# The Down stage of a gated block: H quantised in small parts by VectorE, later tiles turned by DMA in halves

## The chip, the core and the metric

The kernel runs on one core of a Trainium2 chip. The engines named are TensorE (PE, matmuls and transposes), VectorE (DVE), ScalarE (ACT), GpSimd (POOL) and SyncE (SP), which issues the DMAs. The metric is device time of one execution in microseconds, the median of the runs.

## The reference, cut to what matters

```python
x = x + tanh(g_xattn) * matmul(fake_quant(layernorm(x)), fake_quant(ctx))
# the block's second half, on layernorm(x) as A:
gate, up = A @ Wg.T * g, A @ Wu.T * g              # A fp8-quantised, W int4-quantised
h = silu(gate) * up                                # 1024 x 2752
gm = max(max(abs(h)) / (448 * 6), 1e-8)            # one number for all of h
xr = h / gm
# blocks of 16 columns; the last 128 columns are quantised twice
def fp8_block_qdq(v):
    s = max(max(abs(vb)) / 448, 1e-8)              # one per block vb
    return float8_e4m3(vb / s) * s
Am = concat(fp8_block_qdq(xr[:, :n]), q1, q2)      # q1 = qdq(outl), q2 = qdq(outl - q1)
y = Am @ Wd.T * gm                                 # Wd int4-quantised, 1024 wide
out = x + tanh(g_ffn) * y
```

All of h must exist before gm does, and gm before any column of Am. Both index arrays are the identity in the data that is timed; code under `mid_moved > 0` is not executed.

## The kernel before, in words

Rows are worked in 8 tiles of 128. The gate and up products come in column units of 256; in the last unit, eight pieces of H (128x256) are made by TensorE, ScalarE (silu) and VectorE (`make_h`, L1311), and VectorE takes the maxima of blocks of 16 (`max_h`, L1316) into `hm`. H goes to memory by DMA and is read back tile by tile into `h_in` (two slots, `load_tile`, L412).

The Down stage starts when the last maxima are there. VectorE reduces all of `hm` to one number per row (L1407), GpSimd takes the maximum over the partitions (L601), VectorE makes scales from it (L1409 to L1411). Then, for each tile: `scale_h` keeps the outlier columns (L1431) and makes the blocks' scale and coefficient (L1232 to L1235); GpSimd multiplies the tile by the coefficients (`h_times_coef`, L607), except the first 8 groups of 128 columns of tile 0, which VectorE multiplies (L1256); `round_scaled` rounds to fp8 precision with a power of two added and taken off (L1238, L1239, L1240, L1246) and multiplies by the scale (L1247); `quantise_twice` treats the 128 outlier columns (L1263 to L1270).

TensorE turns the quantised tile, 22 transposes of 128x128 (L869) in groups of four into a PSUM bank `tb`; ScalarE copies a group out as f16, the high half (L693), and VectorE subtracts that from the bank, the low half (L1173). `down` then multiplies: 22 column groups, two halves of 512 output columns, three products each (high-high, high-low, low-high), so 132 matmuls a tile (L977). `finish` (L1478) adds the result to the residual, and SP stores it. Tile t+1 is turned between the two output halves of tile t. The order is written out by hand, for each engine; an engine carries out its list in order, and semaphores order the engines: `am_ready` (parts quantised), `lo_done` (groups split), `y_done` (an output half multiplied), `y_out` (result taken, bank free), `turned`, `h_loaded`.

Each step of VectorE's quantisation waits for the one before it on its own semaphore. The transposing DMA is used for the weights already: `turn_gate_up` (L424, 16 blocks of 128x128 f16 per DMA) and `turn_down` (L433, mostly 8).

## Time and profile before

| | us |
|---|---|
| median of 3 runs | 937.62 |
| lowest, highest | 936.37, 938.55 |
| profiled execution | 939.1 |
| its span, first to last instruction | 937.3 |
| busy in the span: TensorE, VectorE | 784.9, 643.9 |
| busy in the span: GpSimd, ScalarE | 337.1, 263.3 |

Shares over the whole span mix stages with different limits; the Down stage is the part from about 646 us to the end. The trace gives each instruction's start and length, what it sat idle for before it, and which engine's event ended that idle time.

### The profile page before, as it was taken

The page shows a single profiled execution, that of the slowest core. Times are in us where ns is not written, and L with a number is a line of the kernel's source. Part 1 is how long each engine was busy: PE and PEld are TensorE (multiplying, and loading weights), DVE is VectorE, ACT ScalarE, POOL GpSimd, SP SyncE. Part 2 cuts the span into 40 slices and gives each one's busy share as a digit, 9 for nine tenths or more (in the row PEclk, how much of TensorE's full clock was granted, in tenths as well). Part 3 has the DMA queues.
Part 4 walks back from the last instruction along what each step waited for, and adds up shares of the span by engine and source line. Part 5 has one row for each costly group of instructions (what it writes and reads, how often), then busy time and mean ns, then how long its engine had stood idle before and what let it go on. Part 6 is the DMA issues. An engine that isn't in the chain of part 4 may idle for free.

```text
span 937.3 us, 11305 instructions
## 1 busy us (share of the span) xinstructions
PE 784.9 (84%) x3808; PEld 377.3 (40%) x3808; DVE 643.9 (69%) x1023; ACT 263.3 (28%) x368; POOL 337.1 (36%) x175
## 2 busy tenths in 40 slices
PE   0698100679999999999999999995589979999998
PEld 0243100445554444444444444442245434444443
DVE  5999789978767566666757667414988695976510
ACT  1964420232235353343425343300001111011000
POOL 1002054854227485665757576500302222112000
PEclk9999555789999999999999999998789999999999
DMA  7633300110038997979788897704011221121100
GB/s 288 209 103 146 130 0 0 45 62 22 20 112 184 214 196 158 221 175 224 169 198 195 194 209 167 176 28 182 1 60 61 106 104 47 60 105 45 45 23 22
DMA packets 144675, 110.32 MB, mean 118 GB/s; under 512 B 117632, under 2 KB 128896, under 8 KB 143616
## 3 DMA queue, kind: packets, MB, share of 16 engines
q1 hardware_dynamic: 144640, 109.88, 44.4%
q8 instruction: 18, 0.29, 0.1%
q14 instruction: 17, 0.14, 0.0%
HBM read 61.88 MB, written 19.66 MB: 87 GB/s over the span
## 4 chain that ended last, share of the span: by engine, by line
PE 69%; DVE 24%; issue 2%; ACT 2%; DMA 1%; POOL 1%; SPq 1%; DVEq 0%; ACTq 0%
PE acc L927 44%; PE acc L977 22%; PE tb L869 2%; DVE mid L1173 2%; DVE big L1240 1%; DVE wbuf L1167 1%; DVE bst L1065 1%; DVE h_in L1247 1%; DVE big L1095 1%; DVE h_in L1239 1%; DMA big<-in_x_dram 1%; DVE h_in L1238 1%; DVE h_in L1185 1%; DVE w_max L1155 1%; DVE h_in L1240 1%
## 5 line engine op out<-in xcount | busy, mean ns | idle before, releaser
L927 PE MATMUL acc<-mid 128*128 128x512 f16 (+1 forms) x2112 | 448.4, 375 | 0.0
L927 PEld LDWEIGHTS acc<-mid 128*128 128x128 f16 x2112 | 207.3, 98 | 239.3 <-issue 1.9
L977 PE MATMUL acc<-big,mid 128*128 128x512 f16 x1056 | 234.6, 385 | 5.2 <-DVE mid L1173 5.2
L544 POOL TENSOR_TENSOR wbuf<-wbuf,w_inv 128x1024 f32<-128x1024 f32 (+1 forms) x68 | 128.4, 1894 | 156.4 <-DVE w_inv L1161 156.4
L977 PEld LDWEIGHTS acc<-big,mid 128*128 128x128 f16 x1056 | 104.4, 99 | 132.6 <-issue 6.8
L583 POOL TENSOR_TENSOR h_in<-wbuf,h_in 128x1024 f16<-128x1024 f32 (+1 forms) x56 | 114.5, 2044 | 87.1 <-ACT h_in L784 86.9
L1311 DVE SCALAR_TENSOR_TENSOR h_out<-acc,gs,silu 128x256 f32<-128x256 f32 (+1 forms) x88 | 41.5, 471 | 119.3 <-ACT silu L742 98.3
L693 ACT ACTIVATE mid<-tb 128x512 f16<-128x512 f32 (+1 forms) x88 | 44.9, 571 | 256.4 <-PE tb L869 234.6
L607 POOL TENSOR_TENSOR h_in<-h_in,mid 128x2752 f32<-128x2752 f32 (+1 forms) x8 | 38.3, 4794 | 166.6 <-DVEq L1438 159.5
L687 ACT ACTIVATE wbuf<-wbuf 128x1024 f32<-128x1024 f32 (+1 forms) x68 | 69.1, 1017 | 99.6 <-POOL wbuf L544 98.8
L1155 DVE TENSOR_REDUCE tb<-wbuf 128x64 f32<-128x1024 f32 (+1 forms) x56 | 65.4, 1169 | 42.0 <-DMA wbuf<-in_L_ffn_w_gate_dram 23.5
L784 ACT ACTIVATE h_in<-wbuf 128x1024 f16<-128x1024 f32 (+1 forms) x56 | 57.1, 1019 | 114.9 <-DVE wbuf L1167 114.9
L1173 DVE TENSOR_TENSOR mid<-tb,mid 128x512 f16<-128x512 f32 (+1 forms) x88 | 51.9, 647 | 45.0 <-ACT mid L693 44.7
L1167 DVE SCALAR_TENSOR_TENSOR wbuf<-wbuf,tb 128x1024 f32<-128x1024 f32 (+1 forms) x56 | 65.1, 1163 | 0.3 <-issue 0.2
L742 ACT ACTIVATE silu<-acc,gs 128x256 f32<-128x256 f32 (+1 forms) x88 | 40.0, 456 | 88.8 <-PE acc L927 88.8
L869 PE MATMUL tb<-ident,big 128*128 128x128 f32 x64 | 10.9, 343 | 57.2 <-DVE big L1270 50.9
L869 PE MATMUL tb<-ident,h_in 128*128 128x128 f32 x176 | 24.6, 287 | 25.6 <-DVEq L1457 16.4
L1478 DVE SCALAR_TENSOR_TENSOR mid<-acc,gs,mid 128x512 f32<-128x512 f32 x16 | 11.5, 748 | 41.2 <-PE acc L977 39.0
L855 PE MATMUL acc<-mid,big 128*128 128x512 bf16 x128 | 32.2, 410 | 4.6 <-DVE big L1095 4.6
L1316 DVE TENSOR_REDUCE hm<-h_out 128x256 f32 (+2 forms) x88 | 34.0, 387 | 2.7
L869 PEld LDWEIGHTS tb<-ident,big 128*128 128x128 f32 x64 | 10.0, 182 | 58.1 <-DVE big L1270 51.5
L869 PEld LDWEIGHTS tb<-ident,h_in 128*128 128x128 f32 x176 | 20.1, 145 | 31.1 <-issue 19.9
(141 smaller groups left out, 594.6 us busy)
## 6 DMA issues: line engine op xcount, KB each, us to landing
h_in<-h_d SPq DMA_DIRECT2D x8, 1376.0 KB, 6.0
wbuf<-in_L_ffn_w_gate_dram SPq DMA_DIRECT2D x21, 512.0 KB, 4.3
wbuf<-in_L_ffn_w_up_dram SPq DMA_DIRECT2D x21, 512.0 KB, 4.1
h_d<-h_out SPq DMA_DIRECT2D x80, 128.0 KB, 3.4
wbuf<-in_L_ffn_w_down_dram SPq DMA_DIRECT2D x16, 512.0 KB, 4.3
wbuf<-in_ctx_dram SPq DMA_DIRECT2D x12, 512.0 KB, 4.4
big<-in_x_dram SPq DMA_DIRECT2D x8, 512.0 KB, 8.2
x_d<-big SPq DMA_DIRECT2D x8, 512.0 KB, 4.0
```

The source lines that it names most:

```text
L544: pool.tensor_tensor(w, w, spread(w_inv[0:rows, b, 0:cols // BLK]), ALU.mult).then_inc(w_scaled, 1)
L583: pool.tensor_tensor(nat[s % 4][:, H:H + cols], wbuf[:, s % 4, 0:cols], nat[s % 4][:, 0:cols], ALU.subtract)\
L687: act.activation(wbuf[0:rows, b, 0:cols], wbuf[0:rows, b, 0:cols], ACT.Copy, bias=MAGIC, scale=W_UP)\
L693: act.activation(dst, tb[bank][:, 0:n * P].rearrange("p (k r) -> p k r", k=n)[:, :, 0:width], ACT.Copy).then_inc(hi_done, 1)
L784: act.activation(nat[s % 4][:, 0:cols], wbuf[:, s % 4, 0:cols], ACT.Copy).then_inc(nat_hi, 1)
L869: last = pe.transpose(tb[bank][:, q * P:q * P + rows], src[0:rows, k * P:(k + 1) * P], ident[0:rows, 0:rows])
L927: last = pe.matmul(acc[m % 4][:, 0:cols], left[:, k, s * P:(s + 1) * P], ring[:, slot, right, k, 0:cols], start=(k == 0 and left is a_hi a ...
L977: last = pe.matmul(acc[2 * i + hf][:], amT[:, i, left, k, :], right[:, k, hf * MW:(hf + 1) * MW], start=(k == 0 and left == 0 and right is ...
L1155: dve.tensor_reduce(top, blocks(wbuf[0:rows, b, 0:cols]), AX_X, ALU.max, apply_absolute_value=True).then_inc(scale_step, 1)
L1167: dve.scalar_tensor_tensor(out=w, in0=w, scalar=MAGIC, in1=spread(block_scale(b, looped)[0:rows, 0:cols // BLK]), op0=ALU.subtract, op1=AL ...
L1173: dve.tensor_tensor(dst, tb[bank][:, 0:n * P].rearrange("p (k r) -> p k r", k=n)[:, :, 0:width], hi, ALU.subtract).then_inc(lo_done, 1)
L1311: dve.scalar_tensor_tensor(out=h_out[:, m % 2, 0:cols], in0=acc[m % 4][:, cols:2 * cols], scalar=gs[:, 2:3], in1=silu[:, m % 2, 0:cols], o ...
```

## The change

Tiles 0 and 1 of the Down stage are quantised in six parts of 3 or 4 column groups (`H_PARTS`), each turned by TensorE, split by ScalarE and VectorE and multiplied before the next. Tiles 2 to 7 are quantised in two halves of 11 groups; ScalarE and VectorE split a half before it is turned, into `nat_h`, and SP turns it with one DMA of 22 blocks. GpSimd's multiplication is gone: VectorE multiplies by the coefficient itself (`start_part`), which is made from the maxima without the global scale and bounded by it in the same instruction. The coefficients of tiles 0 and 1, and the part of the global maximum that is known by then, are worked out during the last H unit.

```diff
-DG = -(-DK // 4)
-C_FIRST = 8
-C_PART = 16
+DH = DK // 2
+H_PARTS = (0, 3, 7, 11, 15, 19, DK)
+DG = len(H_PARTS) - 1
+H_SMALL = 1e-20
...
+        amT = mid[:, 0:2 * DK * P].bitcast(F16).rearrange("p (s g v k r) -> p s g v k r", s=2, g=2, v=2, k=DH)
         o = 2 * DK * P
-        mgh = mid[:, o:o + I]
-        o += I
+        mgh = mid[:, o:o + DH * P]
...
+        nat_h = wbuf[:, :, :].rearrange("p b h -> p (b h)")[:, 0:HPAD].bitcast(F16).rearrange("p (g v n) -> p g v n", g=2, v=2)
...
+            def turn_half(t, i, g):
+                if g == 0:
+                    sp.wait_ge(y_done, 2 * (t - 1))
+                sp.wait_ge(nat_h_lo, halves_before(t) + g + 1)
+                sp.dma_start_transpose(amT[:, i, g, :, :, :].rearrange("p v k r -> p (v k) r"),
+                                       nat_h[:, g, :, :].rearrange("p v n -> p (v n)")).then_inc(h_turned[g], 16)
+            def store_out(t, i):
+                sp.wait_ge(y_out, t + 1)
+                sp.dma_start(out_d[t], x1_t[:, i, :]).then_inc(out_stored[i], 16)
+            for t in range(2):
                 sp.wait_ge(turned, (t + 1) * DG + G_DOWN)
+                load_tile(t + 2, t)
+            for t in range(2, NT):
+                i = t % 2
+                store_out(t - 2, i)
+                turn_half(t, i, 0)
+                sp.wait_ge(out_stored[i], 16 * (t // 2))
+                load_x1(t, i)
+                turn_half(t, i, 1)
+                if t + 2 < NT:
+                    load_tile(t + 2, i)
...
-            def h_times_coef(t, i, start=0):
-                pool.wait_ge(hcoef_ready, t + 1)
-                v = blocks(h_in[:, i, start * P:I])
-                pool.tensor_tensor(v, v, spread(h_coef[:, i, start * P // BLK:NBH]), ALU.mult).then_inc(h_scaled, 1)
-            h_times_coef(0, 0, C_FIRST)
-            h_times_coef(1, 1)
-            with pool.Fori(1, NT // 2) as it:
-                for i in range(2):
-                    h_times_coef(2 * it + i, i)
...
+            for t in range(2):
+                for c in range(DG):
+                    ks = slice(H_PARTS[c], H_PARTS[c + 1])
+                    g = G_DOWN + t * DG + c
+                    hi_part(g, g % 4, amT[:, t, ks.start // DH, 0, ks.start % DH:(ks.stop - 1) % DH + 1, :], ks.stop - ks.start, P)
+            act.wait_ge(nat_lo, UNITS_D * UNIT_PIECES)
+            for t in range(2, NT):
+                for g in range(2):
+                    act.wait_ge(am_ready, parts_before(t) + g + 1)
+                    if t >= 3:
+                        act.wait_ge(h_turned[g], 16 * (t - 2))
+                    act.activation(nat_h[:, g, 0, :], h_in[:, t % 2, g * DH * P:(g + 1) * DH * P], ACT.Copy).then_inc(nat_h_hi, 1)
...
+            def turn_h(t, c):
+                pe.wait_ge(am_ready, t * DG + c + 1)
+                g = G_DOWN + t * DG + c
+                turn_piece(h_in[:, t, :], P, range(H_PARTS[c], H_PARTS[c + 1]), g, g % 4)
...
+            turn_h(0, 0)
+            for t in range(2):
+                for c in range(DG):
+                    pe.wait_ge(lo_done, G_DOWN + t * DG + c + 1)
+                    for hf in range(2):
+                        last = down(t, hf, range(H_PARTS[c], H_PARTS[c + 1]))
+                        if c == DG - 1:
+                            last.then_inc(y_done, 1)
+                        if hf == 0 and t * DG + c + 1 < 2 * DG:
+                            turn_h((t * DG + c + 1) // DG, (c + 1) % DG)
+            for t in range(2, NT):
+                pe.wait_ge(y_out, t - 1)
+                for g in range(2):
+                    pe.wait_ge(h_turned[g], 16 * (t - 1))
+                    for hf in range(2):
+                        last = down(t % 2, hf, range(g * DH, (g + 1) * DH))
+                        if g == 1:
+                            last.then_inc(y_done, 1)
...
+            def coef_unbound(t, i, link):
+                mx, coef = hm[:, t, :], h_coef[:, i, :]
+                link(dve.tensor_scalar(coef, mx, H_SMALL, 1.0 / (FP8_MAX * V_UP), ALU.max, ALU.mult))
+                link(dve.reciprocal(coef, coef))
             for s in range(NT):
                 h_tile(UNITS_D, s)
+                if s == NT - 1:
+                    dve.wait_ge(h_done, (NU + 1) * NT)
+                    step(dve.tensor_reduce(gpart[:, 3:4], h_out[:, s % 2, :], AX_X, ALU.max, apply_absolute_value=True))
+                    dve.tensor_reduce(gmx[:, 1:2], gpart[:], AX_X, ALU.max).then_inc(part_max, 1)
                 h_top(UNITS_D, s)
-            dve.wait_ge(hmax_done, (NU + 1) * NT)
-            dve.tensor_reduce(gmx[:, 1:2], hm[:].rearrange("p t b -> p (t b)"), AX_X, ALU.max).then_inc(part_max, 1)
+                if s in (1, 2):
+                    dve.wait_ge(hmax_done, unit_tile(UNITS_D, s - 1) + 1)
+                    coef_unbound(s - 1, s - 1, step)
+                if s == NT - 2:
+                    dve.wait_ge(hmax_done, (NU + 1) * NT - 1)
+                    before = (UNITS_D + 1) * UW // BLK
+                    dve.tensor_reduce(gpart[:, 0:1], hm[:, 0:s + 1, :].rearrange("p t b -> p (t b)"), AX_X, ALU.max)
+                    dve.tensor_reduce(gpart[:, 1:2], hm[:, s + 1, 0:before], AX_X, ALU.max)
+                    dve.tensor_reduce(gpart[:, 2:3], hm[:, s + 1, before + UW // BLK:NBH], AX_X, ALU.max)
...
+            def scale_h(t, i):
+                step(dve.tensor_scalar(h_scale[:, i, :], hm[:, t, :], gs[:, 7:8], TINY, ALU.mult, ALU.max))
+            def start_part(t, i, ks):
+                cs = slice(ks.start * P, min(ks.stop * P, I))
+                vb, mg = blocks(h_in[:, i, cs]), mgh[:, 0:cs.stop - cs.start]
+                v = h_in[:, i, cs]
+                step(dve.scalar_tensor_tensor(out=vb, in0=spread(h_coef[:, i, cs.start // BLK:cs.stop // BLK]), scalar=gs[:, 6:7], in1=vb,
+                                              op0=ALU.min, op1=ALU.mult))
+                step(dve.tensor_scalar(mg.bitcast(I32), v.bitcast(I32), 0x7F800000, 0x00400000, ALU.bitwise_and, ALU.bitwise_or))
+                step(dve.tensor_scalar(mg, mg, 1.5 * V_UP * 2.0**-6, None, ALU.max))
+            def end_part(t, i, ks):
+                cs = slice(ks.start * P, min(ks.stop * P, I))
+                v, mg = h_in[:, i, cs], mgh[:, 0:cs.stop - cs.start]
+                step(dve.scalar_tensor_tensor(out=v, in0=v, scalar=1.0 / V_UP, in1=mg, op0=ALU.mult, op1=ALU.add))
+                step(dve.tensor_tensor(v, v, mg, ALU.subtract))
+                last = dve.tensor_tensor(blocks(v), blocks(v), spread(h_scale[:, i, cs.start // BLK:cs.stop // BLK]), ALU.mult)
+                if ks.stop == DK:
+                    step(last)
+                    last = quantise_twice(h_in[:, i, I - SELECT:I].unsqueeze(1), ro_h[:, i:i + 1, :], mgh[:, 0:SELECT], step)
+                last.then_inc(am_ready, 1)
...
+            def lo_half(t, i, g):
+                dve.wait_ge(nat_h_hi, halves_before(t) + g + 1)
+                dve.tensor_tensor(nat_h[:, g, 1, :], h_in[:, i, g * DH * P:(g + 1) * DH * P], nat_h[:, g, 0, :], ALU.subtract)\
+                    .then_inc(nat_h_lo, 1)
...
+            for t in range(2):
+                reorder_max(t, t)
+                if t == 1:
+                    keep_h_outliers(1)
+                    scale_h(1, 1)
+                for c in range(DG):
+                    ks = slice(H_PARTS[c], H_PARTS[c + 1])
+                    if t == 0 and ks.stop == DK:
+                        keep_h_outliers(0)
+                    start_part(t, t, ks)
+                    if t == 0 and c == 0:
+                        dve.tensor_scalar(gs[:, 5:6], gs[:, 3:4], th[:, 1:2], W_DOWN, ALU.mult, ALU.mult)
+                        step(dve.tensor_scalar(gs[:, 7:8], gs[:, 4:5], 1.0 / FP8_MAX, None, ALU.mult))
+                        dve.wait_ge(hmax_done, (NU + 1) * NT)
+                        scale_h(0, 0)
+                    elif c > 0:
+                        lo_group(t, c - 1)
+                    else:
+                        lo_group(t - 1, DG - 1)
+                    end_part(t, t, ks)
+            for t in range(2, NT):
+                i = t % 2
+                reorder_max(t, i)
+                coef_unbound(t, i, step)
+                keep_h_outliers(i)
+                scale_h(t, i)
+                if t == 2:
+                    lo_group(1, DG - 1)
+                else:
+                    lo_half(t - 1, 1 - i, 1)
+                finish(t - 2, i)
+                start_part(t, i, slice(0, DH))
+                end_part(t, i, slice(0, DH))
+                start_part(t, i, slice(DH, DK))
+                lo_half(t, i, 0)
+                end_part(t, i, slice(DH, DK))
+            lo_half(NT - 1, 1, 1)
+            finish(NT - 2, 0)
+            finish(NT - 1, 1)
```

VectorE at the start of the Down stage, before (`hm` block maxima, `gmx` maximum per row, `gall` over all partitions, `mid` here the rounding operand):

```order
L1316 TENSOR_REDUCE hm<-h_out 128x16 [waits h_done]
L1407 TENSOR_REDUCE gmx<-hm 128x1 [waits hmax_done]
L1409 TENSOR_SCALAR gs<-gall 128x1 [waits all_max]
L1410 TENSOR_SCALAR gs<-gs,th 128x1 [waits dve_step]
...
L1256 TENSOR_TENSOR h_in<-h_in,mid 128x1024 [waits hs_step]
L1238 TENSOR_SCALAR mid<-h_in 128x1024 [waits qh_step]
L1239 TENSOR_SCALAR mid<-mid 128x1024 [waits qh_step]
L1240 SCALAR_TENSOR_TENSOR h_in<-h_in,mid 128x1024 [waits qh_step]
L1246 TENSOR_TENSOR h_in<-h_in,mid 128x1024 [waits qh_step]
L1247 TENSOR_TENSOR h_in<-h_in,mid 128x1024 [waits qh_step]
```

and in the changed kernel (`gpart`: four partial maxima):

```order
L1406 TENSOR_REDUCE gpart<-h_out 128x1 [waits h_done]
L1407 TENSOR_REDUCE gmx<-gpart 128x1 [waits dve_step]
L1310 TENSOR_REDUCE hm<-h_out 128x16 [waits h_done]
L1423 TENSOR_SCALAR gs<-gall 128x1 [waits all_max]
L1424 RECIPROCAL gs<-gs 128x1 [waits dve_step]
L1425 TENSOR_SCALAR gs<-gs 128x1 [waits dve_step]
...
L1462 SCALAR_TENSOR_TENSOR h_in<-mid,gs,h_in 128x384
L1464 TENSOR_SCALAR mid<-h_in 128x384 [waits dve_step]
L1465 TENSOR_SCALAR mid<-mid 128x384 [waits dve_step]
L1514 TENSOR_SCALAR gs<-gs,th 128x1 [waits dve_step]
L1515 TENSOR_SCALAR gs<-gs 128x1
L1455 TENSOR_SCALAR mid<-hm,gs 128x172 [waits hmax_done,dve_step]
```

The reduction over all of `hm` and the scale and coefficient steps have left this place; the first quantised piece is 384 columns wide instead of 1024, and `hm` of the last piece is taken after the row maximum.

TensorE at a tile in the middle, before (`tb` transposed groups, `acc` the output):

```order
L977 MATMUL acc<-big,mid 128x512 [waits lo_done,y_out]
L977 MATMUL acc<-big,mid 128x512 x65
L869 MATMUL tb<-ident,h_in 128x128 [waits lo_done,am_ready]
L869 MATMUL tb<-ident,h_in 128x128 x3
L869 MATMUL tb<-ident,h_in 128x128 [waits lo_done]
L869 MATMUL tb<-ident,h_in 128x128 x3
...
L869 MATMUL tb<-ident,h_in 128x128
L977 MATMUL acc<-big,mid 128x512 x66
```

and in the changed kernel, from the last part of tile 1 to the second half of tile 2 and on:

```order
L881 MATMUL tb<-ident,h_in 128x128 [waits lo_done,am_ready]
L881 MATMUL tb<-ident,h_in 128x128 x2
L990 MATMUL acc<-big,mid 128x512 x12
L990 MATMUL acc<-big,mid 128x512 [waits lo_done]
L990 MATMUL acc<-big,mid 128x512 x17
L990 MATMUL acc<-big,mid 128x512 [waits h_turned0,y_out]
L990 MATMUL acc<-big,mid 128x512 x65
L990 MATMUL acc<-big,mid 128x512 [waits h_turned1]
L990 MATMUL acc<-big,mid 128x512 x65
```

The transposes between the output halves, with their wait for `am_ready`, have gone from here; each half tile of matmuls waits for a turned half (`h_turned`), and both output halves use it before the next.

SP in the tile loop, before (`h_in<-h_d` the next H tile, `mid<-x_d` the residual):

```order
L495 ISA [waits y_out]
L495 DMA out_dram<-mid 128x1024
L496 ISA
L416 ISA [waits out_stored0]
L416 DMA mid<-x_d 128x1024
L487 ISA
L412 ISA [waits turned]
L412 DMA h_in<-h_d 128x2752
```

and in the changed kernel:

```order
L507 DMA out_dram<-mid 128x1024 [waits y_out]
L501 DMA_TRANSPOSE mid<-wbuf 128x22x128 [waits nat_h_lo,y_done]
L427 DMA mid<-x_d 128x1024 [waits out_stored0]
L501 DMA_TRANSPOSE mid<-wbuf 128x22x128 [waits nat_h_lo]
L423 ISA
L423 DMA h_in<-h_d 128x2752
```

Two transposing DMAs per tile have joined SP's list; the residual's load stands behind the first and the next H load behind the second.

## Rows read from the trace of the kernel before

**Rows 1.** The page: granted TensorE clock in 40 slices; shares of the chain.

```profile
PEclk9999555789999999999999999998789999999999
...
PE 69%; DVE 24%; issue 2%; ACT 2%; DMA 1%; POOL 1%; SPq 1%; DVEq 0%; ACTq 0%
```

**Rows 2.** Timeline, 636 to 712 us: start, length, engine, line, operation, [idle before <-releaser].

```profile
645.87 0.48 DVE L1311 SCALAR_TENSOR_TENSOR h_out<-acc,gs,silu 128x256 f32<-128x256 f32 x1 [4.24 <-ACT silu L742]
...
646.85 1.59 DVE L1407 TENSOR_REDUCE gmx<-hm 128x1 f32<-128x1376 f32 x1
648.57 0.38 POOL L601 PARTITION_ALL_REDUCE gall<-gmx  x1 [47.37 <-DVE gmx L1407]
...
657.32 4.04 DVE L1247 TENSOR_TENSOR h_in<-h_in,mid 128x1024 f32<-128x1024 f32 x1
...
661.66 1.94 PE L869 MATMUL tb<-ident,h_in 128*128 128x128 f32 x8 [16.40 <-DVEq L1457]
...
665.45 11.84 PE L977 MATMUL acc<-big,mid 128*128 128x512 f16 x48 [1.85 <-DVE mid L1173]
...
677.00 0.29 DVE L1263 TENSOR_TENSOR mgo_a<-mgo_a,h_in 128x128 f32<-128x128 f32 x1
...
680.46 2.03 PE L869 MATMUL tb<-ident,h_in 128*128 128x128 f32 x14 [3.17 <-DVE h_in L1270]
```

**Rows 3.** Timeline, later stretches of the Down stage, 684 to 937 us.

```profile
684.14 20.50 PE L977 MATMUL acc<-big,mid 128*128 128x512 f16 x84 [1.64 <-DVE mid L1173]
684.54 0.15 PEld L977 LDWEIGHTS acc<-big,mid 128*128 128x128 f16 x1 [0.27 <-issue]
...
688.72 15.42 PEld L977 LDWEIGHTS acc<-big,mid 128*128 128x128 f16 x72 [0.18 <-issue]
...
740.58 14.42 PE L977 MATMUL acc<-big,mid 128*128 128x512 f16 x66 [1.69 <-DVE mid L1173]
...
856.18 3.05 PE L869 MATMUL tb<-ident,h_in 128*128 128x128 f32 x22
...
933.38 0.75 DVE L1478 SCALAR_TENSOR_TENSOR mid<-acc,gs,mid 128x512 f32<-128x512 f32 x1 [13.43 <-PE acc L977]
```

**Rows 4.** The chain of waits in order of time: start, length, what.

```profile
736.01 0.45 PE tb L869 x4
...
859.23 28.49 PE acc L977 x132
```

**Rows 5.** Busy time in one tile's stretch: length, PE, PEld, DVE, ACT, POOL, clock, DMA.

```profile
824.97:856.34 31.37, 31.27 (x156) 15.29 (x155) 23.22 (x35) 2.94 (x6) 4.88 (x1) 1.00 0.22 80
```

**Rows 6.** Groups by shape, 640 to 940 us: busy, mean ns | idle before.

```profile
L1173 DVE TENSOR_TENSOR mid<-tb,mid 128x512 f16<-128x512 f32 x40 | 24.7, 683 | 41.9 <-ACT mid L693 41.7
...
L693 ACT ACTIVATE mid<-tb 128x512 f16<-128x512 f32 x40 | 21.4, 601 | 221.7 <-PE tb L869 221.7
...
L1247 DVE TENSOR_TENSOR h_in<-h_in,mid 128x2048 f32<-128x2048 f32 x7 | 16.0, 2292 | 0.2
...
L1478 DVE SCALAR_TENSOR_TENSOR mid<-acc,gs,mid 128x512 f32<-128x512 f32 x16 | 11.5, 748 | 41.2 <-PE acc L977 39.0 <-DVE mid L1235 2.2
L1234 DVE RECIPROCAL mid<-mid 128x172 f32<-128x172 f32 x8 | 9.8, 1228 | 0.3
L1239 DVE TENSOR_SCALAR mid<-mid 128x2048 f32<-128x2048 f32 x7 | 8.6, 1227 | 0.2
...
L1247 DVE TENSOR_TENSOR h_in<-h_in,mid 128x704 f32<-128x704 f32 x7 | 6.2, 893 | 0.2
...
L1239 DVE TENSOR_SCALAR mid<-mid 128x704 f32<-128x704 f32 x7 | 3.7, 527 | 0.2
```

**Rows 7.** Transposing DMAs of 16 blocks, L424: landing times.

```profile
DMA to landing us min/median/max: 4.2/4.7/6.5
```

**Rows 8.** Transposing DMAs of line L433, mostly of 8 blocks: landing times.

```profile
DMA to landing us min/median/max: 2.7/3.7/5.8
```

**Rows 9.** DMA issues: count, size of one, median us from issue to landing.

```profile
h_in<-h_d SPq DMA_DIRECT2D x8, 1376.0 KB, 6.0
```

More of the change, by code:

```diff
@@ L983, in _ @@
                 pe.wait_ge(piece_turned[b], turns_before(b, UNITS_D) * 16)
-            for part, groups in enumerate((range(0, C_FIRST // 4), range(C_FIRST // 4, DG))):
-                pe.wait_ge(am_ready, part + 1)
-                turn_h(0, 0, groups)
-                pe.wait_ge(lo_done, G_DOWN + groups.stop)
-                for hf in range(2):
-                    last = down(0, hf, range(4 * groups.start, min(4 * groups.stop, DK)))
-                    if part == 1:
-                        last.then_inc(y_done, 1)
@@ L1464, in _ @@
[L1464 to L1474 removed]
+                    ins.then_inc(q_step, 1)
+                    dve.wait_ge(q_step, count[0])
@@ L1475, in finish @@
+            def finish(t, i):
+                dve.wait_ge(x1_loaded[i], 16 * (t // 2 + 1))
                 for hf in range(2):
@@ L1494, in _ @@
-            scale_h(3, 1, 32)
-            def during(t, i, rounds, quantised=True, scaled=True):
-                before, after = rounds
-                finish(t - 1, 1 - i, before * 16 + 16)
-                lo_h(t + 1, 1 - i, range(DG))
-                if quantised:
-                    for part in range(2):
-                        quantise_h(t + 2, i, part, C_PART)
-                if scaled:
-                    scale_h(t + 3, 1 - i, after * 16 + 16)
-            with dve.Fori(0, (NT - 4) // 2) as it:
-                during(2 * it + 1, 1, (it, it + 2))
-                during(2 * it + 2, 0, (it, it + 2))
```

155 lines of the change are left out of this document (35 added, 120 removed).

## The prediction

> **What bounds the kernel now.** I read the page's chain of waits first, for the engine that sets the end. TensorE holds 69% of it and VectorE 24% [rows 1]; the row of granted clocks beside it [rows 1] shows where TensorE ran below full speed: each digit is 23.4 us, and around the Down stage only digits 28 to 30 (633 to 703 us: 8, 7, 8) sag. Then the timeline of VectorE and TensorE over the hand-over into the Down stage [rows 2]. The reader should see three things there. First, the last H piece is ready at 645.87 + 0.48 = 646.35 us, and TensorE gets its first Down work, transposes, only at 661.66 and its first Down matmul at 665.45: all of tile 0's first 1024 columns must be quantised before one column is turned. Second, while GpSimd multiplies tile 0's other columns, VectorE's product of 1024 columns takes 4.04 us (at 657.32), where 2048 columns of such a product take 2.29 us elsewhere [rows 6]. Third, TensorE waits again, 3.17 us before 680.46. Last, the steady part. One tile there is 22 transposes in 3.05 us and 132 matmuls in 28.49 us (0.2158 us each) [rows 3, 4], and in one whole tile of 31.37 us VectorE is busy for only 23.22 us [rows 5]. So the stage has two limits: VectorE's chain at its start (and once more around 740 to 763 us, where TensorE waited 1.69 us at 740.58 [rows 3]), TensorE from then on.
>
> **The sum, against the profiled execution (939.1 us, span 937.3, last TensorE result taken by VectorE at 933.38 [rows 3]).** I follow TensorE from the last H piece to its last matmul.
>
> Start. The global maximum no longer needs the 1.59 us reduction over all block maxima after the last piece; one over the piece's 256 columns and one over 4 numbers stand there. Their bounds are 0.29 (128 columns) and 1.59 us (1376 columns) [rows 2]; I take 0.45 and 0.2, nearest to the 128-column row, so GpSimd starts about 1.4 us earlier and VectorE goes on at 647.6. Reductions and coefficients for tiles 0 and 1 that now stand inside the last unit fall into VectorE's waits between H pieces, which I cost at nothing. They are two 0.3 us and two 1.23 us operations and one reduction of about 1.4 us, spread over three pieces. If that cover were gone they would cost 3 to 4 us.
>
> After three one-column steps (0.6 us), part 0 of tile 0 has 384 columns. From 704 and 2048 columns [rows 6] an operation with two tensor inputs costs 0.16 us + 1.04 ns per column, and one with a single input 0.16 us + 0.52 ns per column, plus 0.035 us between them. So 384 columns take 0.56 and 0.36 us, and the part takes 1.4 (multiply, two single-input steps), 0.7 (two one-column steps and the scale) and 1.8 us (three two-input steps): ready at 652.1. Transposes start 9.5 us earlier than 661.66. While they and ScalarE's copy run (0.60 us for 512 columns [rows 6]), VectorE does part 1's opening (512 columns: 0.69 + 2 x 0.43 + gaps = 1.65), then the 0.55 us subtraction. First matmul at 654.5, 11.0 us earlier.
>
> Tiles 0 and 1 now go part by part. TensorE's share of a 512-column part is 24 x 0.216 = 5.2 us of matmuls and 4 transposes at 3.05/22 = 0.14 us, 5.7 us. VectorE's is 1.65 + 2.2 + 0.68 = 4.6 us. The dependent path from one part's turning (copy 0.6, subtraction 0.7, closing 2.2: 3.6 us with gaps) is shorter than the 5.2 us that TensorE has work for. So TensorE paces, except at the last part of each tile, where the outlier passes (677.00 to 680.46: 3.4 us [rows 2]) and 320 columns make the path 6.5 us: 1.3 us of stall, twice. Sum from 654.5: 264 matmuls x 0.2158 = 57.0; 41 transposes, 5.7; stalls 2.6; slow clock at the restart 2.3. The last is from the restart at 684.14, where the weight loads come 0.43 us apart (0.27 idle and 0.15 busy, at 684.54) until 688.72, about 11 of them [rows 3], each 0.21 us late; the granted clock of those slices is the 1.2 GHz level mixed with 2.4. Tile 1 ends at 722.1; in the trace of before its last matmul ends at 736.01 [rows 4]. So 14 us are gained by here.
>
> The new hole. Tile 2 no longer goes through TensorE's transposes. Its first half needs, after tile 1's last outlier pass, which ends 6.9 us before tile 1's last matmul (3 transposes 0.4, 12 matmuls 2.6, 18 matmuls 3.9), at 715.2: coefficient, reciprocal (1.23 [rows 6]), outliers and scale, 2.2 together; last subtraction 0.55; two output steps 1.5 (0.748 each [rows 6]); then for 1408 columns the opening 1.63 + 2 x 0.89 + gaps = 3.5 and the closing 5.0; the opening of the second half, 3.4, under which ScalarE's copy hides (1408 columns, at most 2.75 x 0.60 = 1.65 us); subtraction 1.63. That is 733.0. SP then issues the turning DMA. Of a 22-block one there is no row: 8-block ones land in 2.7 to 5.8 us, median 3.7, 16-block ones in 4.2 to 6.5, median 4.7 [rows 7, 8]. Going on along the medians gives 5.5, along the shortest 5.3; the bounds are 4.2 and twice 5.7. I take 5.7, since SP's queue is calm here. Tile 2's matmuls start at 738.7, after 16.6 us without work, and with the slow clock again (2.3 us).
>
> On that landing time the Trainium skill ("DMA: Bandwidth & Descriptors", Latency and other measured facts) gives transposing DMAs an effective 261 GB/s in the non-contiguous case; a half is 0.72 MB, so 2.8 us, and by that the sum would be 2.9 us lower, 914. The rows of this kernel, with the fixed time in them, speak for the longer value.
>
> Steady part. TensorE loses its 22 transposes: 28.49 us a tile instead of 31.37. VectorE's tile is now: 2.2 (coefficient to scale), two subtractions 3.3, output 1.5, four two-input passes over 2752 columns 4 x (2.29 + 0.89) = 12.7, two single-input passes 2 x (1.23 + 0.53) = 3.5, outliers 3.4, gaps 0.4: 27.1 us. Against before's 23.22 it gains GpSimd's multiplication and keeps the subtractions. That is 1.4 us under TensorE's 28.5. The half's subtraction writes 2-byte numbers from SBUF, which has no row; at the PSUM rate (0.683 for 512 columns [rows 6]) both cost 0.5 more, still under. Each half lands at least 3 us before it is wanted (tile 3's first half: 733.0 + 27.1 + 5.7 = 765.8, wanted at 738.7 + 2.3 + 28.5 = 769.5), and the lead grows by 1.4 us a tile. Behind SP's new waits for a half stand the residual's load and the next H load (6.0 us [rows 9]); the first has 25 us, the second 20 us before VectorE asks. TensorE ends at 738.7 + 2.3 + 6 x 28.49 = 911.9, against 933.4. What follows the last matmul is unchanged. The difference is -21.5 us; some twelve hand-overs on the path (0.13 us from VectorE's 648.44 to GpSimd's 648.57 [rows 2]) give back about 1 us. 939.1 - 20.5 = 918.6 for such an execution; the median shown is 1.5 us lower (937.62), so 917.
>
> **The rivals.** (a) The halves land late: twice 5.7 us. For it: SP holds loads, stores and turnings in one queue, and 16-block ones have taken 6.5. Against: no load runs just then. Only the hole grows (steady slack is 3 us and more, and shifts along): 923. (b) VectorE becomes the bound. It needs 1.4 us more per tile; with both half subtractions at twice their cost a tile is 30.4 us, TensorE's last half starts near 906 and the kernel takes about 925. For: 27.1 is near 28.5, and every wait of VectorE for ScalarE or SP adds. Against: all its long operations have rows. (c) Slower than before: TensorE stays at the 1.2 GHz level through the piecewise tiles 0 and 1, since it now stops at 12 hand-overs. Price 253 matmuls x 0.21 = 54 us, 971; it decides once 97 matmuls beyond my 22 run slow. For: the clock sagged after 3.17 + 1.64 us of waiting around 680 to 684. Against: after 1.69 us at 740.58, 66 matmuls ran in 14.42 us, full rate [rows 3], and I expect no stop above 1.5 us. The same side is reached if a turned half took over 15.5 us (12 of them in a row).
>
> **How the numbers follow.** What this measurement can tell from no change is about 0.2%, 2 us. My forecast, TensorE-paced with one hole, 0.72, its own range 912 to 922 (landing 2.8 to 8, slow clock 1 to 4 us, stalls 1 to 5). (a) 0.10, (b) 0.09, (c) 0.05; 0.04 for several costs that together eat the gain, half of it above the time before. Faster 0.91, same 0.02, slower 0.07. Range 911 to 927: it takes in (a), (b) at its price, and leaves out (c).
>
> **What would show it.** Right: TensorE's transposes of H at about 652, matmuls from 654 to 655; 5.5 to 6 us per part; one hole of 15 to 18 us near 722; then intervals of 28.5 us without waits; VectorE waiting about 1 us per tile at the output step. Wrong: a second hole at a later tile (landings or VectorE late), VectorE without a wait in the last tiles (b), a granted clock near 0.5 between 655 and 720 (c), or turned halves landing after more than 8 us (a).

## The result: 1% faster, and 11 us of the forecast gain missing at the other end of the program

The changed kernel takes 927.60 us (median of 4 runs, 926.29 to 928.49), the kernel before in the same measurement 937.09 us (4 runs, 936.37 to 938.55). The ratio is 0.9896, with a 95% interval of 0.9878 to 0.9913. That is 9.5 us gained, where 20 were forecast, and 0.6 us beyond the upper end of the range.

The profiled execution has a span of 926.0 us, against 937.3. I read it the way the prediction was worked out, from the last H piece on. This is the timeline of the changed kernel (start, length, engine, line, operation, [idle before <- releaser]), in the places that answer to [rows 2, 3]:

```profile
657.74 0.48 DVE L1305 SCALAR_TENSOR_TENSOR h_out<-acc,gs,silu 128x256 f32<-128x256 f32 x1 [2.52 <-ACT silu L746]
658.25 0.42 DVE L1406 TENSOR_REDUCE gpart<-h_out 128x1 f32<-128x256 f32 x1
658.71 0.16 DVE L1407 TENSOR_REDUCE gmx<-gpart 128x1 f32<-128x4 f32 x1
659.00 0.38 POOL L618 PARTITION_ALL_REDUCE gall<-gmx  x1 [49.28 <-DVE gmx L1407]
...
664.30 0.87 PE L881 MATMUL tb<-ident,h_in 128*128 128x128 f32 x3 [7.17 <-DVE h_in L1473]
...
666.42 4.02 PE L990 MATMUL acc<-big,mid 128*128 128x512 f16 x9 [1.25 <-DVE mid L1167]
...
681.74 5.34 PE L990 MATMUL acc<-big,mid 128*128 128x512 f16 x24
...
693.90 0.55 PE L881 MATMUL tb<-ident,h_in 128*128 128x128 f32 x3 [1.21 <-DVE h_in L1264]
...
726.21 0.55 PE L881 MATMUL tb<-ident,h_in 128*128 128x128 f32 x3 [1.20 <-DVE h_in L1264]
...
743.65 3.31 SPq L501 DMA_TRANSPOSE mid<-wbuf  x1
...
748.96 173.14 PE L990 MATMUL acc<-big,mid 128*128 128x512 f16 x792 [15.73 <-DMA mid<-wbuf]
...
922.14 0.75 DVE L1499 SCALAR_TENSOR_TENSOR mid<-acc,gs,mid 128x512 f32<-128x512 f32 x1 [6.30 <-PE acc L990]
```

The reader should see two things. The Down stage looks as it was drawn: the first parts at once, two stalls of 1.2 us behind the outliers, one hole of 15.73 us before tile 2, and then 792 matmuls in one row, without a wait. And all of it is late: the last H piece is ready at 658.22 us, where it was at 646.35 before [rows 2]. From there to VectorE's first look at the last result it takes 263.9 us, against 287.0 before [rows 2, 3]. So the stage gained 23.1 us, and what stands ahead of it lost 11.9. The sum is -11.2; the spans differ by 11.3. (The medians differ by less, 9.5 us, because the profiled execution of before, 939.1 us, lies 2 us above its median.)

What stands ahead is code that the change does not touch. The loss is whole after 23 us. The timeline of GpSimd and VectorE at the start, of the kernel before:

```profile
1.08 0.14 POOL L517 IOTA iot<- 128x8 int32 x1 [0.65 <-POOLq L1527]
...
6.11 0.17 DVE L1041 TENSOR_TENSOR neq<-idx,iot 128x8 f32<-128x8 int32 x1 [6.11 <-DMA idx<-in_L_ffn_ri_mid_dram]
...
9.09 0.37 POOL L538 PARTITION_ALL_REDUCE nall<-nfl  x1 [5.65 <-issue]
...
10.95 10.03 DVE L1065 BATCH_NORM_STATS2 bst<-big 128x6 f32<-128x512 f32 x16
```

and of the changed kernel:

```profile
8.29 0.13 POOL L534 IOTA iot<- 128x8 int32 x1 [7.85 <-issue]
...
10.04 0.17 DVE L1035 TENSOR_TENSOR neq<-idx,iot 128x8 f32<-128x8 int32 x1 [10.04 <-POOL h_in L547]
...
21.16 0.37 POOL L555 PARTITION_ALL_REDUCE nall<-nfl  x1 [10.51 <-issue]
```

GpSimd waits 7.85 us for nothing that the profile shows before the first instruction of its list (four small memsets of constants, at 0.25 us, run ahead of it in both kernels), and 10.51 us before its all-reduce of the two flags. VectorE, in order, waits for these flags before it starts the LayerNorm statistics (10.95 before, 23.03 now).

The same "issue" wait stands in the trace of before at the three places where GpSimd goes from ordinary instructions to an all-reduce or back and no other engine keeps it waiting longer (5.65, 6.99 and 7.16 us); here before the multiplication of H that the change removes:

```profile
656.11 4.16 POOL L607 TENSOR_TENSOR h_in<-h_in,mid 128x1728 f32<-128x1728 f32 x1 [7.16 <-issue]
```

The Trainium skill ("GPSIMD Engine Reference", 2.1 Instruction dispatch) names such a wait: GpSimd's kernels are loaded at run time, and the first call of a freshly loaded one pays about 6 us with no instruction in the profile. These rows agree in kind, and show 5.65 to 10.51 us.

That gave theory A: the loaded code is carried from one execution to the next. The kernel before ends on a multiplication, so its next execution begins with ordinary code loaded. The changed one ends on an all-reduce; its next execution has to load back first, and then load the all-reduce's code while the inputs are being transferred.

### The profile page after: what moved, and what is told of

It is laid out like the page before. It is cut to its first block, busy times and chain, and to the rows that moved or that the text cites. A ratio compares the mean times of both kernels' runs of the same rounds, so it can differ in the third digit from the quotient of the medians.

```text
span 926.0 us, 10779 instructions
## 1 busy us (share of the span) xinstructions
PE 763.7 (82%) x3676; PEld 361.8 (39%) x3676; DVE 666.2 (72%) x1060; ACT 263.5 (28%) x344; POOL 298.7 (32%) x167
## 4 chain that ended last, share of the span: by engine, by line
PE 28%; issue 25%; DVE 24%; POOL 17%; ACT 3%; DMA 2%; SPq 1%; POOLq 0%; DVEq 0%; ACTq 0%
PE acc L990 23%; POOL wbuf L561 8%; POOL h_in L600 8%; DVE wbuf L1161 2%; PE acc L939 2%; DVE bst L1059 2%; PE tb L881 2%; DVE big L1234 1%; DVE w_max L1149 1%; DVE h_in L1233 1%; DVE h_in L1232 1%; DVE big L1089 1%; DVE h_in L1179 1%; DMA wbuf<-in_L_ffn_w_down_dram 1%; ACT h_in L788 1%
## 5 line engine op out<-in xcount | busy, mean ns | idle before, releaser
L990 PE MATMUL acc<-big,mid 128*128 128x512 f16 x1056 | 234.1, 384 | 17.0 <-DMA mid<-wbuf 15.7
L827 ACT ACTIVATE wbuf<-h_in 128x1408 f16<-128x1408 f32 x12 | 16.5, 1377 | 145.0 <-DVE h_in L1473 74.8
L697 ACT ACTIVATE mid<-tb 128x512 f16<-128x512 f32 (+2 forms) x52 | 28.0, 575 | 98.0 <-PE tb L881 76.1
L1167 DVE TENSOR_TENSOR mid<-tb,mid 128x512 f16<-128x512 f32 (+2 forms) x52 | 32.2, 654 | 12.6 <-ACT mid L697 12.3
L841 PE MATMUL tb<-identb,h_in 128*128 128x128 bf16 x64 | 6.6, 265 | 40.0 <-DVE h_in L1125 40.0
L1155 DVE RECIPROCAL w_inv<-tb 128x64 f32<-128x64 f32 (+1 forms) x56 | 30.2, 539 | 1.9
```

The source lines that it names most:

```text
L990: last = pe.matmul(acc[2 * i + hf][:], amT[:, i, k // DH, left, k % DH, :], right[:, k, hf * MW:(hf + 1) * MW], start=(k == 0 and left == ...
```

## The experiments

All are measured against the kernel before on the same chip, whose median there was 935.9 to 936.4 us.

**1. Load back at the end.** One more instruction on GpSimd, after its last:

```
  pool.partition_all_reduce(gall[:, 1:2], gmx[:, 1:2], P, RMAX).then_inc(all_max, 1)
+ pool.iota(iot[:, 0:8], pattern=[[1, 8]], base=0, channel_multiplier=8)
```

> The changed kernel with one instruction more: GpSimd, after its last instruction (the all-reduce of the largest value of H), makes the 128x8 index numbers once more, which nobody reads. Theory A (GpSimd's loaded code is carried from one execution to the next: the changed kernel ends on an all-reduce, so the next execution pays a load of 7.85 us before its first instruction, and the all-reduce of the flags loads its own code only after that, while the inputs' transfers run, 10.51 us in place of 5.65): GpSimd pays the load near 661 us, beside VectorE and TensorE, the first instruction of the program starts at about 1.1 us again, the all-reduce of the flags at 9.1, the LayerNorm statistics at 11.0, all that follows is 11.6 to 12.1 us earlier, and the time is 927.6 - 11.9 = 915.7 us (915 to 916.5). Rival B (the later start comes of where or how long GpSimd's program is, or of the other engines' programs being fetched at the same time): 927.6 us, and the first GpSimd instruction stays at 8.3. Rival C (the input transfers alone slow the code load): the first instruction stays at 8.3 too, since no transfer runs before it in either kernel.

Measured: 915.55 us (5 runs, 914.39 to 915.72), ratio 0.9782 (0.9768 to 0.9795). One instruction that computes nothing gives 12 us. Its timeline:

```profile
1.08 0.14 POOL L534 IOTA iot<- 128x8 int32 x1 [0.64 <-POOLq L1556]
...
9.19 0.37 POOL L555 PARTITION_ALL_REDUCE nall<-nfl  x1 [5.77 <-issue]
...
652.06 0.87 PE L882 MATMUL tb<-ident,h_in 128*128 128x128 f32 x3 [7.18 <-DVE h_in L1474]
...
654.18 4.02 PE L991 MATMUL acc<-big,mid 128*128 128x512 f16 x9 [1.25 <-DVE mid L1168]
654.28 0.13 POOL L619 IOTA iot<- 128x8 int32 x1 [7.14 <-issue]
...
736.38 172.97 PE L991 MATMUL acc<-big,mid 128*128 128x512 f16 x792 [15.73 <-DMA mid<-wbuf]
```

The load now stands at 647 to 654 us, where nobody waits for GpSimd (7.14 us), and the start is that of the kernel before.

**2 and 3. The two controls.** In the second, the changed kernel gets one more instruction at the same place, but of the kind that is already loaded. In the third, the kernel before is made to end as the changed one does.

```
+ pool.partition_all_reduce(nall[:], nfl[:], P, RMAX)      # at GpSimd's end, in either
```

> The changed kernel with one GpSimd instruction more at its end, as in the run before this one, but of the same kind as the last: the all-reduce of the flags a second time. Theory A: the code that GpSimd is left with is the all-reduce's again, nothing changes: 927.6 us, first GpSimd instruction at 8.3 us, flags' all-reduce at 21.2. Rival B (length or place of GpSimd's program): it should move by as much as the run before this one, to about 916 us if that one does.

> The kernel before, with the all-reduce of the flags issued once more as GpSimd's last instruction, after its last multiplication of the Down stage. Nothing else of it is changed. Theory A: the next execution finds the all-reduce's code loaded and starts as the changed kernel does: first GpSimd instruction at 8.3 us in place of 1.08, flags' all-reduce at 21.2 in place of 9.1, first TensorE instruction at 38.9 in place of 27.3, and 937.1 + 11.6 = 948.7 us. Rivals B and C: 937.1 us, within 1.

Measured: the changed kernel with it 927.10 us (4 runs), ratio 0.9904 (0.9889 to 0.9919), no difference from 0.9896. The kernel before with it 948.44 us (4 runs), ratio 1.0132 (1.0116 to 1.0147): 12.5 us slower by an instruction after all its other GpSimd work. The loss is all ahead of the Down stage (GpSimd's maximum of H comes at 661.04 us, where it came at 648.57), and its start is the changed kernel's:

```profile
8.31 0.13 POOL L517 IOTA iot<- 128x8 int32 x1 [7.87 <-issue]
...
21.58 0.37 POOL L538 PARTITION_ALL_REDUCE nall<-nfl  x1 [10.91 <-issue]
```

So rival B (length and place of the program) is out, and C with it: the kind of the last instruction decides, in both kernels and in both directions. That the thing carried over is loaded code is theory A's reading: no profile shows a load, only the waits. It fits the starts of all twelve profiles, 0.64 to 0.65 us behind an ordinary last instruction and 7.85 to 7.94 behind an all-reduce.

**4. Why the second load takes twice as long.**

```
+ sp.wait_ge(flag_step, 5)
  for t in range(NT):
      sp.dma_start(x_all[:, t, :], x_d[t]).then_inc(x_loaded[t], 16)
```

> The changed kernel (which ends on the all-reduce) with the loads of x and of the context held until the flags' all-reduce has run, so that no large transfer runs while GpSimd's code is loaded. Theory A with its second half (the load of the all-reduce's code takes 10.51 us in place of 5.65 because the x and context transfers fill the queues): the first GpSimd instruction stays at 8.3, the flags' all-reduce comes 5.7 us after it is asked for, near 16.4 us in place of 21.2; the statistics then wait for x, which is asked for at 16.8 (the first load of x landed within about 6 us of its issue in the kernel before): they start near 21 and end within 2 us of where they end now, total 925 to 930 us. If the second load is long for another reason, the all-reduce stays at 21.2, x comes after it and the total is 932 to 934 us.

Measured: 927.37 us (one run, one profile). The timeline:

```profile
8.31 0.13 POOL L535 IOTA iot<- 128x8 int32 x1 [7.88 <-issue]
...
16.52 0.37 POOL L556 PARTITION_ALL_REDUCE nall<-nfl  x1 [5.85 <-issue]
...
20.28 1.29 DVE L1060 BATCH_NORM_STATS2 bst<-big 128x6 f32<-128x512 f32 x2 [1.81 <-DMA big<-in_x_dram]
```

With no input transfer in flight the second load takes 5.85 us in place of 10.51: the transfers cost it 4.7 us. The first load keeps its 7.88 us, so it was never disturbed by them. The total hardly moves because x now lands later: the statistics end at 31.17 us in place of 32.64, and the spans are 925.6 and 926.0.

**5. What the turning by DMA is worth.** With the closing instruction of the first experiment, all eight tiles take the way of tiles 0 and 1:

```
- for t in range(2):                 # tiles turned in parts by TensorE
+ for t in range(8):
- for t in range(2, NT):             # turn_half, hi and lo of a half: not used
```

> The changed kernel with GpSimd's closing instruction (as in the first experiment, 915.55 us there), and with no tile turned by DMA: tiles 2 to 7 are turned by TensorE in parts of 3 to 4 groups and split from PSUM, as tiles 0 and 1 are. So the small parts, VectorE alone and the ready factors stay, the turning by DMA goes. Theory (as the prediction has it: DMA turning saves the transposes, 0.44 us for each of 6 parts, 2.6 us a tile, but pays one hole of 15.7 us before tile 2, of which a first part turned by TensorE needs 4): 4.0 + 6 x 2.6 = 19.6 us in place of 15.7, so 915.6 + 3.9 = 919.5 us less what is hidden, range 917 to 921. Rival D (VectorE, with some 28.5 to 30 us a tile in this form, does not keep up with 31.1 us of TensorE, and the 1.2 us stall of tiles 0 and 1 behind the outliers comes back in each of the six): 6 x 1.2 more, 926 us or over. Rival E (the turning by DMA was worth its 2.9 us a tile in full): 915.6 + 17 = 933.

Measured: 934.87 us (11 runs), ratio 0.9983 (0.9973 to 0.9992). My expectation of 919.5 was wrong by 15 us; rival E named the right size, D the right kind of cause. The timeline around tile 2 to 3 shows it:

```profile
722.06 4.05 PE L997 MATMUL acc<-big,mid 128*128 128x512 f16 x18
...
749.14 0.55 PE L888 MATMUL tb<-ident,h_in 128*128 128x128 f32 x3 [1.20 <-DVE h_in L1273]
749.52 2.75 PE L997 MATMUL acc<-big,mid 128*128 128x512 f16 x12
...
753.66 2.12 PE L997 MATMUL acc<-big,mid 128*128 128x512 f16 x9 [1.38 <-DVE mid L1176]
...
756.62 0.55 PE L888 MATMUL tb<-ident,h_in 128*128 128x128 f32 x3 [0.85 <-DVE h_in L1482]
757.01 4.05 PE L997 MATMUL acc<-big,mid 128*128 128x512 f16 x18
```

A tile takes 757.01 - 722.06 = 34.95 us: 3.43 are three waits for VectorE at the tile's end (1.20, 1.38 and 0.85), and 31.52 are work, 28.49 of it products and the other 3.0 transposes. The busy times of this stretch (length, PE, PEld, DVE, ...):

```profile
722.06:757.01 34.95, 31.52 (x157) 15.19 (x155) 29.71 (x61) 3.37 (x6) 0.00 (x0) 1.00 0.20 72
```

VectorE is busy for 29.7 of them, so a sum of busy times says it keeps up. It does not, because the two engines wait for each other by turns. In the middle of a tile VectorE waits for a copy of what TensorE has just turned, and TensorE turns only between products. At its end TensorE waits for the outliers, the split, and the next tile's factors. Neither gets ahead of the other. The list of VectorE's waits over the eight tiles puts a number on its side (us in total, times, longest):

```profile
DVE mid L1176 <- ACT mid L702: 31.6, 29, 2.0
```

So the way that tiles 2 to 7 take in the changed kernel brought 934.87 - 915.55 = 19.3 us (medians from two chips). From tile 2's first matmul to VectorE's look at the last result it is 929.48 - 722.06 = 207.4 us here and 909.39 - 736.38 = 173.0 in the first experiment. Of these 34.4 us 16.8 are TensorE's waits for VectorE (7.2 for the outliers, 5.4 for the split, 4.2 for the next tile's first part), and the other 17.6 are nearly all transposes; 14.3 come back because tile 2 starts that much earlier without the hole. And the other half of the change alone, small parts by VectorE, gains next to nothing over the kernel before (0.9983): tile 2's first product stands at 722.06 us against 740.58 [rows 3], 18.5 earlier, but from there to the last result it takes 207.4 us against 192.8, and loses 14.6 of them. One thing this experiment does not part: it turns by TensorE and it quantises tiles 2 to 7 in six parts in place of two halves. Larger parts turned by TensorE were not tried, so the 19.3 us are the worth of both together.

**6. The hole's length is VectorE's order.** Only for tile 2:

```
- finish(0); start_part(g0); end_part(g0); start_part(g1); lo_half(g0); end_part(g1)
+ start_part(g0); end_part(g0); finish(0); lo_half(g0); start_part(g1); end_part(g1)
```

> With GpSimd's closing instruction again. In tile 2 alone VectorE's order is changed: the first half's six passes, then the output of tile 0, the subtraction that splits the first half, and only then the second half's first three passes (they stood ahead of the subtraction, the output of tile 0 ahead of all). Theory (the hole before tile 2 is the chain of six passes, the copy, the subtraction and the transposition, and its length is set by VectorE's order alone): the subtraction ends at 740.45 - 11.9 = 728.5 in place of 731.0, by 1.40 + 1.68 us less that wait of the copy: the transposition is issued 2.6 to 3.2 us earlier, the hole is 12.5 to 13.1 in place of 15.73, the second half is then needed 2.5 to 3.2 earlier than now and lands within 0.7 of that; total 915.6 - 2.6 = 913.0 (912.3 to 913.6). Rival (the second half, which VectorE cannot bring earlier, takes it back as a stall within tile 2): 915.0 to 915.6, with a wait of over 1.5 us in the middle of tile 2.

Measured: 911.71 us (5 runs), ratio 0.9735 (0.9720 to 0.9750).

```profile
727.99 3.31 SPq L501 DMA_TRANSPOSE mid<-wbuf  x1
...
733.29 172.73 PE L991 MATMUL acc<-big,mid 128*128 128x512 f16 x792 [12.55 <-DMA mid<-wbuf]
```

The hole is 3.18 us shorter, within the 12.5 to 13.1 expected, nothing is given back, and the spans (913.2 and 909.9) differ by 3.3. The median is 0.6 us below the range that I had given; the medians differ by 3.8, from two chips, which is within the two intervals.

**7. Is the rest of the stage really without a wait?**

```
+ for again in range(2):
      sp.dma_start_transpose(amT[:, i, g, ...], nat_h[:, g, ...]).then_inc(h_turned[g], 16)
+     sp.wait_ge(h_turned[g], 32 * (t - 2) + 16 * (again + 1))
```

> With GpSimd's closing instruction again, and each of the twelve transpositions by DMA issued twice, the second when the first has landed, so that a half is there some 5.2 to 5.6 us later. Theory (as predicted: only the first half of tile 2 is waited for, later halves land with more slack than that; the row of VectorE's readiness for tile 3 says 757.65 + 10.5 = 768.2 against 741.7 + 28.9 = 770.6): the hole grows from 15.73 to 21.1 and the six tiles follow without a wait: 915.6 + 5.4 = 921.0 us (920 to 922). Rival (a) of the prediction (halves land late once and again): each of five more tiles waits too, 5.4 us or part of it, 925 to 947 us.

Measured: 921.60 us (4 runs), ratio 0.9839 (0.9820 to 0.9858).

```profile
741.73 174.32 PE L993 MATMUL acc<-big,mid 128*128 128x512 f16 x792 [20.89 <-DMA mid<-wbuf]
```

Twelve transpositions took twice as long, and only the first is seen: the hole grows by 5.16 us, and the 792 matmuls still run without a wait. They take 1.35 us longer in all, and the clock accounts for most of it: of the second 4 us behind the hole 0.75 was granted, and 15 matmuls ran, where the first experiment had 1.00 and 20. My expectation told rival (a) of the prediction wrongly: (a) said that with halves landing after twice 5.7 us only the hole grows, to 923 us, some 6 more. That is what happened here (921.60 - 915.55 = 6.0 us). So this run bears (a)'s price out; what rules (a) out for the changed kernel is its own landing time, 5.1 to 6.9 us.

**8. Take the wait away rather than the load.** The flags' comparison moves behind the fourth x tile's statistics, and the wait for the all-reduce behind the second tile of the quantisation; GpSimd still starts with both loads.

```
- dve.wait_ge(idx_loaded, 32) ... dve.wait_ge(flag_step, 5); dve.tensor_copy(flag[:], nall[:])
  for t in range(NT):
      dve.wait_ge(x_loaded[t], 16)
      last = stats(t)
+     if t == 3:  the comparison
  ...
+ if t == 1:  dve.wait_ge(flag_step, 5); dve.tensor_copy(flag[:], nall[:]).then_inc(flags_ready, 1)
```

> The changed kernel without the closing instruction: GpSimd still has to load code first (first instruction at 8.3 us). VectorE's comparison of the indices is moved into the middle of the LayerNorm statistics (after x tile 3), and its wait for the flags' all-reduce and the copy of the flags to after the second tile of the attention's quantisation. Nothing of the Down stage is touched. Theory (the 11.9 us were lost only because VectorE waits in order, ahead of the statistics, for an all-reduce that sits behind two loads of code, and nothing else at the start needs them): the statistics start when x lands, near 8.0 (3.4 us after its issue at 4.64), and end near 19.5 in place of 32.6; 13.1 us less than the changed kernel: 927.6 - 13.1 = 914.5 us (914 to 915.5), though both loads are still there. Rival (a load of code at the start holds another engine too, or the weights' loads wait for the flags): 918 to 927.

Measured: 914.62 us (5 runs, 913.09 to 916.23), ratio 0.9770 (0.9753 to 0.9787).

```profile
8.21 1.29 DVE L1048 BATCH_NORM_STATS2 bst<-big 128x6 f32<-128x512 f32 x2 [1.04 <-DMA big<-in_x_dram]
8.38 0.13 POOL L534 IOTA iot<- 128x8 int32 x1 [7.94 <-issue]
...
20.44 0.37 POOL L555 PARTITION_ALL_REDUCE nall<-nfl  x1 [9.69 <-issue]
...
32.41 0.16 DVE L1134 CAST flag<-nall 128x2 int32<-128x2 f32 x1
```

Both loads are there at full length (7.94 and 9.69 us), and they cost nothing that can be measured (0.9770 here, 0.9782 with the closing instruction). The flags are ready at 20.8 us and read at 32.4. The statistics now wait for x, so the start is about as short as the transfers let it be.

**9 and 10. Together.** The ninth has the edits of 1, 6 and 8. The tenth adds that tile 2's block factors are worked out in tile 1's fourth part:

```
+ if t == 1 and c == 3:
+     coef_unbound(2, 0, step)
  lo_group(t, c - 1)
```

> Three edits together: GpSimd's closing instruction, VectorE's flags after the statistics, and tile 2 split first. The closing instruction and the late flags answer the same loss, so only the larger of the two counts: against the profiled run with the late flags alone (span 911.3) this one should be shorter by the hole's 3.2 us and nothing else, span 908.1, time 910.0 us (909.2 to 911). If the two start edits added up, it would be 11 us less, 899; if the shorter hole did not survive with the other start, 913 to 914.6.

> The kernel of the ninth experiment, and in it the block factors of tile 2 (a 0.25 and a 1.23 us instruction) worked out in tile 1's fourth part, where VectorE waits 1.3 to 1.7 us for ScalarE's copy, and not between tile 1 and tile 2, where TensorE waits for VectorE. Theory (the hole is VectorE's chain from tile 1's last pass to the split, and this takes 1.46 us out of it, while in tile 1 it stands in a wait): hole 12.55 - 1.4 = 11.1 us, time 1.4 us under the ninth's, 908.6. Rival (in tile 1 it delays the part's end and the parts behind it, so that TensorE waits there, or the outliers' end comes later by as much): no change, 910.0.

Measured: the ninth 910.89 us (5 runs), ratio 0.9732 (0.9715 to 0.9749), span 908.4; the tenth 910.93 us (5 runs), ratio 0.9728 (0.9712 to 0.9744), span 908.1. The two cannot be told apart. They and the sixth are the fastest kernels of this study, 24.5 to 25.5 us below the kernel before and about 15 below the changed one by the ratios. Against the sixth alone (0.9735) the late flags add nothing that can be measured. The tenth's hole and products:

```profile
730.78 173.46 PE L991 MATMUL acc<-big,mid 128*128 128x512 f16 x792 [11.63 <-DMA mid<-wbuf]
```

and the ninth's:

```profile
731.75 172.77 PE L991 MATMUL acc<-big,mid 128*128 128x512 f16 x792 [12.56 <-DMA mid<-wbuf]
```

The hole got 0.93 us shorter where 1.4 was expected, and tile 1's end did not come later, so the rival's reason is not the right one. Two others show. Behind tile 1's outliers VectorE now reaches the last split too early, and waits for ScalarE's copy, which it did not in the ninth:

```profile
713.31 0.56 DVE L1169 TENSOR_TENSOR mid<-tb,mid 128x384 f16<-128x384 f32 x1 [0.66 <-ACT mid L698]
```

And 0.69 us is lost again in the products. The busy times of the first 8 us behind the hole say where (the number before the last two is the granted clock); the ninth:

```profile
731.75:735.75 4.00, 4.00 (x11) 1.49 (x12) 3.79 (x7) 0.00 (x0) 0.00 (x0) 0.57 0.28 112
735.75:739.75 4.00, 4.00 (x20) 1.83 (x19) 3.66 (x12) 1.38 (x1) 0.00 (x0) 1.00 0.00 0
```

and the tenth:

```profile
730.78:734.78 4.00, 4.00 (x10) 1.43 (x11) 3.79 (x7) 0.00 (x0) 0.00 (x0) 0.50 0.30 120
734.78:738.78 4.00, 4.00 (x19) 1.69 (x17) 3.65 (x12) 1.38 (x1) 0.00 (x0) 0.90 0.00 0
```

TensorE restarted earlier, but its clock rose from the 1.2 to the 2.4 GHz level later after the restart (0.50 and 0.90 granted, against 0.57 and 1.00). These are single profiles; whether it does so each time was not tried.

## Why the prediction was wrong, by its own steps

The times from the last H piece's end, which is where the prediction starts its sum:

| step | predicted | changed kernel |
|---|---|---|
| first transposes | 5.8 | 6.1 |
| first Down matmul | 8.2 | 8.2 |
| end of tile 1 | 75.8 | 75.0 |
| hole before tile 2 | 16.6 | 15.7 |
| first matmul of tile 2 | 92.4 | 90.7 |
| last matmul | 265.6 | 263.9 |

**The start of the stage** held: the reductions inside the last unit hid in VectorE's waits, and the new maximum took 0.42 + 0.16 us where 0.65 was put. **Tiles 0 and 1** held: 5.6 us a part, stalls of 1.21 and 1.20 us where 1.3 was put. **The hole** was put 0.9 us too long, of which the landing is 0.4 (first matmul 5.31 us after the issue, where 5.7 was put). The rate in the Trainium skill ("DMA: Bandwidth & Descriptors", Latency and other measured facts), 261 GB/s, makes an estimate of 2.8 us for the landing, and was farther off: a half of 0.72 MB took 5.1 us at least. **The steady part** held: no wait in six tiles, VectorE busy for 25.7 us of each 26.6 us that it works on one, where 27.1 was put:

```profile
756.68:783.28 26.60, 26.60 (x125) 12.06 (x124) 25.70 (x33) 2.75 (x2) 0.00 (x0) 1.00 0.62 148
```

The hand-overs, put at 1 us, did not show. VectorE's wait at the output step, put at about 1 us a tile, was not there at first and came late in the stage, with 0.77, 1.79 and 2.50 us. **The rivals** did not come about: (a) because no half took over 6.9 us to land; (b) because TensorE never waited behind tile 2's first half; (c) because from 676 us on, 24 products took 5.34 us, the full rate.

**What failed is the first sentence of the sum, "I follow TensorE from the last H piece to its last matmul".** It takes the last H piece as standing at 646.35 us, as in the trace of before; the code ahead of it is indeed the same, and yet it came at 658.22. With it failed the price of taking away GpSimd's multiplication, which was counted only as work given to VectorE. That multiplication had a second effect: it was the last thing that GpSimd did, and its wait of 7.16 us for code, hidden under VectorE's first passes, was what let the next execution begin at 1.08 us. With it gone the wait moved to the start, where VectorE stands behind it (GpSimd's first instruction 7.2 us later), and pushed the all-reduce's own wait into the inputs' transfers (10.51 us in place of 5.65, 4.9 more). The statistics start 12.1 us later by this, and 11.9 are left at the last H piece. Experiment 1 gives the prediction its missing premise, and then comes out at 915.55 us against the 917 forecast, with the first transposes at 652.06 (652.1 forecast) and the first Down matmul at 654.18 (654.5).

Some of that agreement is luck. As ratios to the kernel before, 0.9782 measured and 0.978 forecast are the same; but in the profiles the stage gained 23.1 us where 20.5 were forecast. The hole, tiles 0 and 1 and the hand-overs had all been put too high, and the profiled execution of before was a long one.

The rows were there to be read. Three waits marked "issue" of 5.65 to 7.16 us on GpSimd, always between an all-reduce and something else, raise the question which of them a removed instruction had been paying for. I had read GpSimd only where it worked.

One of the prediction's reasons was incomplete though its number was right. It gave TensorE's transposes as all that the turning by DMA saves in the steady part. In experiment 5, without it and in six parts a tile, the two engines wait for each other in every tile, and the whole change gains about nothing (0.9983) even with the start mended. So it also parts the two engines; how much of that larger parts alone would do is open.

## What to carry to other kernels

A kernel's first microseconds can depend on how its last execution ended: when an edit removes an engine's last instruction, ask what that engine is left with, and whether the first instruction of the program can use it. If an engine has to load code, end its program on the kind with which it begins, or let nobody wait for it early. And where two engines hand parts back and forth, busy times don't tell whether one keeps up; look for waits that alternate, and for a form in which one of them may run ahead.

## What the runs showed of the hardware that I had not expected

- What GpSimd executed last outlasts the execution. Ending on an all-reduce costs 7.85 to 7.94 us before the first iota of the next one (5 profiles), ending on an iota or a multiplication 0.64 to 0.65 (7 profiles).
- The wait before the flags' all-reduce was 5.65 to 5.85 us where it began before the inputs' transfers (or without them), and 9.69 to 11.13 us where it began while they ran (6 profiles and 4). Before the all-reduce that closes experiment 3, in the middle of the Down stage, it was 6.73 us.
- The load, if it is one, does not wait for the instruction's own input. In the ninth experiment GpSimd was free from 3.42 us on, the flags' input was ready at 13.95, and the all-reduce ran at 14.09, with no wait left.
- A transposition by DMA of 22 blocks in SBUF, 0.72 MB, held SP's queue for 3.31 us and landed after 5.2 us (12 of them in the changed kernel, 5.1 to 6.9):

```profile
DMA to landing us min/median/max: 5.1/5.2/6.9
```
